# Q, K and V projections as a stage of their own instead of inside the attention loop, in a post-LN transformer layer on eight cores

## What is computed

```python
Q = (X @ Wq.T + bq).reshape(B, S, H, d_head) * scale
K = (X @ Wk.T + bk).reshape(B, S, H, d_head) * scale
V = (X @ Wv.T + bv).reshape(B, S, H, d_head)
scores = jnp.where(causal, einsum('bqhd,bkhd->bhqk', Q, K), -inf)
out = einsum('bhqk,bkhd->bqhd', softmax(scores), V) @ Wo.T + bo
x = layernorm(X + out)
x = layernorm(x + (silu(x @ Wg.T) * (x @ Wu.T)) @ Wd.T)   # W = (wq - 128) * s
```

## Time and profile before

| | us |
|---|---|
| median of three runs | 9704.75 |
| the three runs | 9704.75, 9710.64, 9068.95 |
| the profiled execution | 9063.52 |
| its span on the slowest core | 9062.0 |
| spans of the eight cores | 9026.4 to 9062.0 |
| granted TensorE clock over the span, core by core | 0.897 to 0.899 |

### The profile page before, as it was taken

How to read it: one execution, slowest core, us unless ns; L and a number is a source line. 1 busy time by engine, 2 the same in 40 slices (tenths; PEclk the granted TensorE clock), 3 DMA queues, 4 the chain that set the end, 5 groups by cost and what they waited for, 6 DMA issues and landing times. The chain is left out here.

```text
span 9062.0 us, 109015 instructions; the slowest of 8 cores (9026.4 to 9062.0 us)
## 1 busy us (share of the span) xinstructions
PE 7181.7 (79%) x40980; PEld 3609.0 (40%) x40980; DVE 2362.9 (26%) x4914; ACT 2429.3 (27%) x2382; POOL 633.0 (7%) x1188
## 2 busy tenths in 40 slices
PE   5777767596999989964767676767667899998994
PEld 2333333342444434422444444444433344444442
DVE  1222222244443320011121212121224433441001
ACT  1222222222222210012434343434332222220003
POOL 0000000101111100000000000000010111110000
PEclk9888888798999999986989898988888999999997
DMA  4111111314444435655000101010031544442666
GB/s 69 24 27 25 28 27 25 60 56 153 157 157 151 150 108 202 226 185 125 15 21 13 24 13 24 13 24 13 13 70 42 189 150 150 157 157 106 215 216 213
DMA packets 164628, 859.06 MB, mean 95 GB/s; under 512 B 27517, under 2 KB 44157, under 8 KB 99609
## 3 DMA queue, kind: packets, MB, share of 16 engines
q1 hardware_dynamic: 73498, 591.96, 18.7%
q0 software_dynamic: 90624, 260.12, 11.1%
HBM read 759.70 MB, written 176.16 MB: 103 GB/s over the span
## 5 line engine op out<-in xcount | busy, mean ns | idle before, releaser
L233 PE MATMUL ps_s_h<-xth_h,wsl_h 128*128 128x512 bf16 x6144 | 1396.4, 387 | 257.3 <-DMA wsl_h<-wk_hr 257.2
L645 PE MATMUL ps_g_h<-avt,w_g_h 128*128 128x512 bf16 x5632 | 1281.6, 381 | 34.6 <-DVE w_u_h L609 18.5
L652 PE MATMUL ps_u_h<-avt,w_u_h 128*128 128x512 bf16 x5632 | 1273.0, 379 | 0.0
L721 PE MATMUL ps_d_h<-wd_bf_h,gu_sl_h 128*128 128x512 bf16 x5632 | 1224.6, 380 | 42.1 <-DMA gu_sl_h<-gu_s 42.1
L248 ACT ACTIVATE expS_h<-ps_s_h,c_all_h 128x1024 bf16<-128x1024 f32 (+1 forms) x1152 | 1174.9, 1066 | 276.8 <-PE ps_s_h L218 275.2
L267 PE MATMUL ps_av_h<-vaug_h,expS_h 128*128 128x129 bf16 x8704 | 714.3, 225 | 587.0 <-ACT expS_h L248 291.2
L233 PEld LDWEIGHTS ps_s_h<-xth_h,wsl_h 128*128 128x128 bf16 x6144 | 603.1, 99 | 972.5 <-issue 311.6
L267 PEld LDWEIGHTS ps_av_h<-vaug_h,expS_h 128*128 128x128 bf16 x8704 | 560.5, 100 | 840.5 <-issue 788.5
L645 PEld LDWEIGHTS ps_g_h<-avt,w_g_h 128*128 128x128 bf16 x5632 | 552.7, 98 | 706.8 <-issue 48.1
L721 PEld LDWEIGHTS ps_d_h<-wd_bf_h,gu_sl_h 128*128 128x128 bf16 x5632 | 550.5, 98 | 702.6 <-issue 47.9
L652 PEld LDWEIGHTS ps_u_h<-avt,w_u_h 128*128 128x128 bf16 x5632 | 551.1, 98 | 664.4
(11 more groups left out here) (94 smaller groups left out, 3980.3 us busy)
## 6 DMA issues: line engine op xcount, KB each, us to landing
gu_sl_h<-gu_s SPq DMA_DIRECT2D x128, 1408.0 KB, 6.8
wi_stage_h<-wgt_r SPq DMA_DIRECT2D x88, 1024.0 KB, 5.0
wi_stage_h<-wut_r SPq DMA_DIRECT2D x88, 1024.0 KB, 7.4
wdi_h<-wdt SPq DMA_DIRECT2D x88, 1024.0 KB, 8.3
wd_s<-wdc_h POOLq DMA_DIRECT2D x352, 128.0 KB, 2.4
gu_s<-gu_t_h POOLq DMA_DIRECT2D x352, 128.0 KB, 2.1
wd_bf_h<-wd_s SPq DMA_DIRECT2D x16, 2816.0 KB, 14.5
x_tok_h<-xtok SPq DMA_DIRECT2D x32, 1024.0 KB, 4.8
```

The costliest lines, as they stand in the source:

```text
L233: P.op("tensor", lambda E, u=u, off=off, cix=cix, par=par, pj=pj: E.matmul(ps_s[par][:, u * 512:(u + 1) * 512], wsl[pj][:, cix * 128:(cix ...
L645: P.op("tensor", lambda E, cix=cix, pp=pp, qt=qt, b=b: E.matmul(ps_g[pp][:], w_g[b][:, cix * 128:(cix + 1) * 128], avt[:, cix * S_half + q ...
L652: P.op("tensor", lambda E, cix=cix, pp=pp, qt=qt, b=b: E.matmul(ps_u[pp][:], w_u[b][:, cix * 128:(cix + 1) * 128], avt[:, cix * S_half + q ...
L721: P.op("tensor", lambda E, ci=ci, u=u, hc=hc, g3=g3, h5=h5, dset=dset: E.matmul(ps_d[dset + u][:], gu_sl[g3 % 3][:, ci * 512 + u * 128: ci ...
```

## The change

- A new phase p1, once for each half, ahead of everything else. It loads the half of X as before, and the three weights whole: each in two halves of 8 DMAs of 1 MB float32, cast to bf16, into three buffers `w_half` in turn. It makes K, V and Q for all heads, one projection after the other: 16 x 4 groups of 16 matmuls of 128 x 512, evicted by ScalarE in pieces of 512 columns and stored to `kt_s`, `vt_s` and `qt_s` (SyncE's queue, 0.5 MB each). A half of a weight may overwrite its buffer only when the projection that read it is over; TensorE starts a projection when both halves have landed.
- Both p1 phases come first; p2 of hp 0 follows p1 of hp 1.
- p2 loads K, V and Q of each head from the scratch tensors into four sets of buffers, up to three heads ahead. The items "prep" are gone.
- The scores are two items ahead of the exp. The first scores of a head wait for `c_all` (`c_rdy2`).
- The squares move from VectorE to ScalarE: Q first, then all of K, into one larger `sqtmp`, issued behind the exp of the head before. The sums over partitions follow without a break, 8 for hp 0 and 12 for hp 1.
- A block of `vaug` is 130 wide instead of 129.
- p4c has two input and two output buffers and one set of statistics instead of three each.
- The host hands over the three weights transposed and whole, not cut by head.

```diff
+            def p1(P, hp):
+                for cix in range(NCH):
+                    P.dma("gpsimd", xth[:, cix * S_half:(cix + 1) * S_half],
+                          xt_d[cix * 128:(cix + 1) * 128, hp * S_half:(hp + 1) * S_half],
+                          inc="x_ld")
+                xc = P.C["x_ld"]
+                for pj, (scr, w_d, bias_t, scaled) in enumerate(projs):
+                    gpj = P.C["p1_w5"]
+                    for lo in range(2):
+                        h5 = gpj + lo
+                        need = ((h5 - 3) // 2 + 1) * NCH * nqt
+                        P.wait("gpsimd", "p1_mm", min(need, P.C["p1_mm"]) if h5 >= 3 else 0)
+                        for cq in range(NCH // 2):
+                            cix = lo * (NCH // 2) + cq
+                            P.dma("gpsimd", w_half[h5 % 3][:, cq * D:(cq + 1) * D],
+                                  w_d[cix * 128:(cix + 1) * 128, :], inc=f"w_ld{h5 % 3}")
+                        P.op("gpsimd", lambda E: None, inc="p1_w5")
...
+                    for ec in range(NCH):
+                        for qt in range(nqt):
...
+                            if ec == 0 and qt == 0:
+                                P.wait("tensor", f"w_ld{gpj % 3}", W_RDY0)
+                                P.wait("tensor", f"w_ld{(gpj + 1) % 3}", W_RDY1)
...
+                            P.wait("tensor", "p1_ev", P.C["p1_ev"] - 1)
+                            for cix in range(NCH):
...
+                                P.op("tensor", lambda E, cix=cix, cq=cq, wb=wb, ec=ec, pp=pp, qt=qt: E.matmul(
+                                    ps1[pp][:],
+                                    wb[:, cq * D + ec * 128: cq * D + ec * 128 + 128],
+                                    xth[:, cix * S_half + qt * 512: cix * S_half + qt * 512 + 512],
...
+                for h in range(H):
+                    hb = h % 4
+                    P.wait("sync", "head_done", P.C["head_done"] - 3)
+                    P.wait("sync", "sq_k", P.C["sq_k"] - 3)
+                    P.dma("sync", k_sb[hb][:], kt_s[h * 128:(h + 1) * 128, 0:SK], inc=f"kv_ld{hb}")
+                    P.dma("sync", vt_sb[hb][:], vt_s[h * 128:(h + 1) * 128, 0:SK], inc=f"kv_ld{hb}")
+                    P.dma("sync", q_sb[hb][:], qt_s[h * 128:(h + 1) * 128, hp * S_half:(hp + 1) * S_half], inc=f"kv_ld{hb}")
...
+                    P.op("scalar", lambda E, hb=hb: E.activation(sqtmp[:, 0:S_half], q_sb[hb][:], AF.Square),
+                         inc="sq_q")
+                    P.op("scalar", lambda E, hb=hb: E.activation(sqtmp[:, S_half:S_half + SK], k_sb[hb][:], AF.Square),
+                         inc="sq_k")
...
+                    emit_scores(0)
+                    if len(glist) > 1:
+                        emit_scores(1)
+                    for i in range(len(glist)):
+                        if i + 2 < len(glist):
+                            emit_scores(i + 2)
+                        emit_av(i)
...
-            r2 = [sb4(f"r2_{i}", [128, D], F32) for i in range(3)]
+            r2 = [sb4(f"r2_{i}", [128, D], F32) for i in range(2)]
...
-                P.wait("sync", "o_done", P.C["o_done"] - 2)
+                    P.wait("sync", "o_done", P.C["o_done"] - 1)
```

More of the change, by code:

```diff
@@ L168, in build_program @@
+        if debug_stop == "p1":
+            return nc
         avt = sb("avt", [128, NCH * S_half], BF16)
@@ L222, in fill @@
                                 start=True, stop=True),
-                                inc=("it_fill" if jj == len(grp) - 1 else None))
-                    else:
-                        _, h, pj, pr = item
-                        P.wait("tensor", f"wslld{pj}")
-                        if P.C["x_ld"] == XRDY:
-                            P.wait("tensor", "x_ld", XRDY)
-                        nu = prw // 512
-                        for u in range(nu):
-                            off = pr * prw + u * 512
-                            for cix in range(NCH):
-                                P.op("tensor", lambda E, u=u, off=off, cix=cix, par=par, pj=pj: E.matmul(
-                                    ps_s[par][:, u * 512:(u + 1) * 512],
-                                    wsl[pj][:, cix * 128:(cix + 1) * 128],
-                                    xth[:, cix * S_half + off: cix * S_half + off + 512],
-                                    start=(cix == 0), stop=(cix == NCH - 1)),
-                                    inc=("it_fill" if (u == nu - 1 and cix == NCH - 1) else None))
@@ L240, in consume @@
-                def consume(item):
-                    par = P.C["it_done"] % 3
-                    P.wait("scalar", "it_fill", P.C["it_done"] + 1)
-                    if item[0] == "score":
-                        _, h, hb, qt, gi2, nk, grp = item
-                        if qt == 0 and grp[0] == 0:
-                            P.wait("scalar", "c_rdy2")
-                        P.wait("scalar", "av_grp", last_av[par])
+                                inc=("sc_grp" if jj == len(grp) - 1 else None))
@@ L259, in consume @@
                                     inc=("mask_done" if (jj, ks) == dmask[-1] else None))
-                        P.wait("tensor", "it_done")
+                        P.wait("tensor", "exp_done")
                         if dmask:
@@ L439, in p2 @@
                     P.op("vector", lambda E: E.memset(rec[:, 0:1], 0.0), inc="head_done")
-                if hp == 0:
-                    for pr in range(npair):
-                        for par2 in range(2):
-                            P.wait("gpsimd", f"kst{pr}_{par2}")
-                            P.wait("gpsimd", f"vst{pr}_{par2}")
             return p2
@@ L788, in finish @@
                 P.wait("gpsimd", "o_st0")
                 P.wait("gpsimd", "o_st1")
-                P.wait("gpsimd", "o_st2")
-            return emit_chunk, finish
+            return p4c
         for hp in range(2):
@@ L837, in build_program @@
             with ExitStack() as c4:
-                ln2_emit1, ln2_fin1 = make_ln2(hp, c4)
-                def p4c(P, e=ln2_emit1, f=ln2_fin1):
-                    for qc in range(nqc):
-                        e(P, qc)
-                    f(P)
+                p4c = make_p4c(hp, c4)
                 P.phase(f"p4c_h{hp}", p4c)
```

400 lines of the change are left out of this document (180 added, 220 removed).

## The result

| | before | after |
|---|---|---|
| lowest execution, us | 9064.59 | 8912.61 |
| the profiled execution, us | 9063.52 | 8914.09 |
| its span on the slowest core, us | 9062.0 | 8912.5 |
| granted TensorE clock over the span, core by core | 0.897 to 0.899 | 0.890 to 0.893 |
| ratio of times, with its 95% interval | | 0.9825 [0.9812, 0.9839] |

The change makes the kernel 1.75% faster. In some executions of either kernel the clock of one die, or of both, was lower and the time up to 13% longer, which has nothing to do with the change, so all comparisons here are between executions without that (the medians over all, 9267.86 and 8915.28 us, are not comparable).

A forecast was written before the change was run, and what follows sets the result against it. TensorE near full in the feed-forward net, 4 to 7 tenths in most of p2; projections and attention fall from 4220 to 1693 + 868 + 1478 = 4039 us, p4c gives 30 back: 9063.5 - 151 = 8912, rounded 8910; range 8790 to 9560.

The forecast's parts named there:

- first matmul after the first load: Start of p1: 16 loads of X and 16 of a weight, 109 us before the first matmul; bounds 90 to 131.
- a pause inside p1: TensorE waits for a half weight whose buffer was in use: 29.8 us, twice in a half; bounds 26 to 35.
- TensorE busy in one p1: One half's 3072 matmuls of 128 x 512 at p4a's 0.2167 us each: 665.8 us.
- prologues: Start of each head in p2: squares hidden on ScalarE, reduces without a break; 15.2 us for hp 0, 21.8 for hp 1.
- bodies: Each head's attention loop in p2, scores two items ahead: 31.8 us for hp 0, 63.1 for hp 1.
- p2 of hp 0, of hp 1: 16 heads of transposes, prologue and body, plus the first K, V and Q: 868 us and 1478 us.
- p4c, two of them, above before: p4c with two buffers: 7 us a chunk with waits, 15 us more per half, 30 in all; bounds 0 and 102.
- what a measurement can tell: Whole kernel: a result within 2% is about what a measurement can tell from no change; chance 0.53.
- The second item of lead buys nothing: Rival, p2's bodies: they stay at 75.5 and 36.0 us, 266 us more, 9176; chance 0.12.
- The clock: Rival, p1: dense projections on all cores run at clock 0.84, 238 us more, 9148; chance 0.11.
- The lower clock lasts longer: Rival, p2: 12 us more of each body run at 1.2 GHz, half lost, 190 us, 9100; chance 0.10.
- More than I count: Rival, p2: hp 1 bodies at their floor and square root's table load moved ahead, together 161 us, 8749; chance 0.17.

The follow-up runs named there:

- e5: The changed kernel with p1's weights loaded in slices of one head into four buffers, instead of halves into three: 8678.82 us.
- e4: The changed kernel with p4c as before the change: three input buffers, three output buffers, three sets of statistics: 8849.94 us.
- e1: The changed kernel with the scores one item ahead again, nothing else: 9188.49 us.
- e9: The changed kernel with weight slices, second X loaded early and three-buffer p4c, plus dummy matmuls at heads' starts and ends: 8529.91 us.
- e8: The kernel before with items two ahead, squares on ScalarE, and dummy matmuls in the prologue and transposes: 8461.28 us, ratio 0.9343.

## Why the prediction was right or wrong

| step, us | predicted | measured |
|---|---|---|
| first matmul after the first load | 109 | 106 |
| a pause inside p1 | 29.8 (26 to 35) | 31.7, 31.5, 33.0, 32.1 |
| TensorE busy in one p1 | 665.8 | 670.8, 669.4 (665.7 in e5) |
| p1, both halves | 1693 | 1689 |
| prologues | 15.2, 21.8 | 15.3, 22.4 |
| bodies | 31.8, 63.1 | 30.4, 62.7 |
| p2 of hp 0, of hp 1 | 868, 1478 | 853, 1478 |
| p4c, two of them, above before | 30 | 53 |
| the profiled execution | 8910 | 8914.09 |

**The time was right, and most steps with it.** The pitch of the weight loads, taken from the 17th in line, gave start and pauses within 4 us. The dense matmul of p4a gave p1's busy time within 5; in e5, which has no pauses inside, the same matmuls take 665.7 us, 0.1 off, so the 5 belong to the stretches after each pause. The pace of ScalarE gave the body of hp 1 within 0.4. That the sum came within 4 us is in part luck: p1 came out 4 us shorter and p2 of hp 0 15 shorter (its bodies 1.4 us each, of the 2.1 that I had given back at changes of `qt`), and p4c 23 longer.

**The mis-sized term: p4c.** I let one load in two share the DMA engines with a store and took 6.8 us a chunk, 7 with waits. It was about 7.8 a chunk (6.1 + 53 / 32): the load landed after 8.5 us, not 6.1, and ScalarE waited 77.3 us for loads against 24.9 with three buffers (e4). The 53 us are inside the bounds I gave, 0 and 102 for the two stages.

**The step that failed: what a measurement can tell.** The prediction called everything within 2% "about what a measurement can tell from no change" and put 0.53 there. The interval of the ratio is 0.9812 to 0.9839, so 1.75% is told from nothing: it is more than ten times the half width of the interval. The three times shown, 9704.75, 9710.64 and 9068.95, had led me to take their spread for the uncertainty. It is not: the executions of the kernel before that can be compared, 9064.59 to 9092.96, agree to 0.3%. For the same reason the upper end of the range, 9560, made from 9551 for a median that falls as the first one did, answered no open question of the kernel. And the forecast of -1.7% holds only against the profiled execution: against the median, 9704.75, the same 8910 would be a fall of 8.2%; like compared with like, there is none.

**The rivals.** *The second item of lead buys nothing*: e1 is that case, 9188 where I put 9176, and the change is 276 us from it. *The clock*: p1 ran at 1.00 but for the stretches around the pauses, 0.95 over all, and at 1.00 from end to end in e5, on all eight cores, so the 238 us never came. The Trainium skill ("TensorE: Matmul & The Clock Gate", section "Seeing it yourself") says that three cores of a die in dense matmuls take the die to 13/16; the executions compared here don't show it, neither in p1 (1.00 in e5) nor in p4a (0.99). *The lower clock lasts longer*: p2 of hp 0 did run at a mean clock of 0.71 (before 0.84), and a body's mean clock of 0.83 means some 10 us of it at 0.50, close to the 12 of that rival. But its price, 6 us a head, was too high: e9, which removes a third of it in hp 0 and nearly all in hp 1, gains 0.3 and 1.8 us a body. For a third of hp 0's body TensorE waits, and what waits loses little by a low clock. What the two thirds that stay in hp 0 cost, no run shows. *More than I count*: the bodies of hp 1 at 62.7 are far from 55.4, and the table load for the square root stayed. The squares got one only at the first square of each half, in place of the one that the first eviction had before:

```profile
L333 ACT ACT_TABLE_LOAD x30 | 38.5, 1283 | 633.1 <-DVE nrm_h L330 633.1
L297 ACT ACT_TABLE_LOAD x2 | 2.6, 1283 | 37.5 <-DMA q_sb_h<-qt_s 37.5
```

The Trainium skill's rule on this ("ScalarE: Activation LUTs", section "Table sets: the hidden batching unit"), that cheap functions are in every set, agrees with this trace: 30 loads for 32 heads' square roots, as in the earlier trace rows. The section names relu, copy, identity and abs; that it holds for the square too is what this trace adds.

**Where the gain comes from, I had half right.** The prediction said that nearly all of it was hp 1's, 17.5 us a head; it is 4.4 + 12.8 = 17.2 by the stages. It did not say what the experiments show: that the separate stage stands in the way of the lead's full worth. I had compared the changed bodies with the last heads' bodies and the projections with dense work, which is right for one item of lead and hides that the merged form gains at least as much from the second item, and in hp 0 nearly twice as much (9.9 us a head with projections, 5.2 in the last head without).

## What to carry to other kernels

- When a change has several parts, price each as if it came alone on the kernel before. Here a single one, two items of lead, was worth 407 us by itself, more than twice the whole change.
- A long block of work put between short dependent ones fills pauses only if enough of the short ones are ahead. Compare the idle time of the bound engine with and without the block: equal idle time (14.8 and 13.6 us here) says that it fills nothing. Where the other engine sets the pace, put the block behind the loop; where TensorE waits for a change of banks, spread it.
- Read the uncertainty of a comparison from executions that can be compared, not from the spread over all, and forecast against one of them.

## What the runs showed of the hardware

- TensorE's clock can be held up by matmuls whose result nobody reads. The stretch with transposes, sums and the wait for `c_all` ran at 0.50; with dummies the prologue and the body after it stood at 1.00 (e8). It paid where TensorE is busy (2.3 us a body of hp 0 with projections, 59 of 65 us busy) and hardly where it waits (0.3 us, 20 of 30 us busy, e9).
- A cast load of 1 MB of float32 to bf16 follows the last one after 3.2 us on all eight cores at once: 32 of them in the 106 us before p1's first matmul, 17 in e5's first 58 (an estimate from these two stretches, less the 6.7 us in which a single slice lands).
- With all eight cores at the same work, 3072 matmuls of 128 x 512 took 665.7 us on the slowest core, 0.2167 us each, and the granted clock was 1.00 (2.4 GHz) on all eight (e5).
- Loads and stores of 1 MB: with three buffers for each a load takes 10.9 to 11.2 us and the stretch moves 291 to 295 GB/s, with two 8.5 us and 237 to 242 GB/s. The shorter latency is no sign of a better use.
